# FFN1's end with its updates between quarters of the last block, and a prologue in which k's first tile and x's high parts stand ahead of q's split on ScalarE

## The chip, the cores and the metric

The kernel runs on one core of one Trainium2 chip. The metric is device time in microseconds (us), the median of several executions. Engines are called as in the profile: PE (TensorE matmuls) with PEld (its weight loads), DVE (VectorE), ACT (ScalarE), POOL (GpSimd) and SP (SyncE, which issues the DMAs). Each engine works through its own list of instructions in order and waits on semaphores that the others raise.

## The reference

x is 8 blocks of 128 tokens by 512 features, ctx a second input of the same shape. Four residual layers follow one another, all in float32:

```python
x = x + L0_xattn(layernorm(x), ctx, Wq, Wk, Wv, Wo)     # keys and values from ctx and x, 16 heads of 96
x = x + L0_ffn(layernorm(x), ...)
x = x + L1_xattn(layernorm(x), ctx, Wq, bq, Wkv, bkv, Wo, bo)   # 32 heads of 128
x = x + L1_ffn(layernorm(x), W, b, A, Bmat, LiMEs)

def L1_ffn(x, W, b, A, Bmat, LiMEs):
    H = x @ W.T + b                                   # 512 wide
    z = x @ A                                         # rank 32
    H_slice = H[:, odd tokens, :8]
    delta_slice = z[:, odd tokens] @ LiMEs.T
    logits = 0.5 * H_slice / max|H_slice| + 0.5 * delta_slice / max|delta_slice|
    probs = softmax(logits)
    weights = probs * sigmoid((probs - second_largest(probs)) / 0.5)
    weights = weights / (sum(weights) + 1e-9)
    p_mix = repeat(weights, 2) @ LiMEs                # one weight row for each pair of tokens
    return H + ((z * p_mix) @ Bmat) * 0.5
```

## The kernel before

Tokens lie in 8 blocks of 128. Every float32 matrix product is made as three products of float32r parts: a value is split into a high part (a copy on ACT) and a low part (value minus high part, on DVE or POOL), and PE adds hi x hi, lo x hi and hi x lo in one bank of PSUM. So one 128x128 weight tile against 512 columns is three matmuls (lines 603 to 605), and a full product over 512 features is twelve.

**The prologue** runs from the launch to the first attention head. SP loads, in this order: the first k and v weights (kv_raw), ctx (into qT, in four pieces), x's blocks 0 to 3, the identity and the gate weights, x's blocks 4 to 7, the first q weights (eight pieces, `load_q`, line 526 and 528). ACT splits ctx into cT_hi, DVE and POOL make cT_lo. PE then projects ctx on k and v (`project_context`, four uses u = 0 to 3 of four PSUM banks; u even is k, u odd is v), one k-step at a time for the first two quarters of ctx and with both last quarters at once for the rest. Between these uses it transposes the normalised blocks of x (`transpose_x`, line 831). A block of x goes through: statistics (DVE, line 1677 to 1681), rstd (POOL, line 1421), shift (DVE, line 1686, minus mean times rstd), `normalise_x` (ACT, line 1221), `transpose_x` (PE), `norm_hi` (ACT, line 1226, writes xT_hi), `norm_lo` (DVE, line 1698, writes xT_lo). When blocks 0 to 3 have xT_lo and the bank of context use 0 is evacuated ("kv", 0: ACT lines 1031 and 1043, two instructions), PE projects x on k and v ("kv", 4 and 5), then transposes blocks 5 and 6 and projects on q ("q", 0 to 2). The q weights are split on ACT (line 1020, q0_hi) and POOL (line 1344, q0_lo).

**FFN1's end.** `big_h(b)` makes one block of H (twelve matmuls, four k-steps "quarters" of three); H's blocks 0 to 3 are added to x by `add_h`, those of 4 to 7 stay in PSUM. `z_half` makes z and H's first 8 features, `small` (line 988) the logits of the odd tokens. DVE and ACT then turn logits into weights in a chain of small instructions (lines 1848 to 1892). PE transposes the weights (line 997, wT), multiplies them by LiMEs (line 1001, pmix), DVE multiplies with z (line 1900, zp), ACT and DVE split zp (lines 1333, 1334 and 1906), and PE makes the eight updates ("delta", line 1009): for blocks 4 to 7 into the bank that holds H's block, for 0 to 3 into banks ov and pt in turn. DVE adds an update to x (line 1914), except for blocks 6 and 7, which ACT copies to SBUF (line 1337, moved) and POOL adds (line 1513). SP stores each block of 256 KB when it is added (lines 587, 590 and 593). The order of the updates is written out in one tuple:

```python
DELTAS = (6, 7, 4, 5, 0, 1, 2, 3)
BY_DVE = DELTAS[2:]
```

The loops over heads between these two stretches are not touched.

## Time and profile before

| | us |
|---|---|
| median of 3 runs (lowest, highest) | 1126.47 (1125.64, 1127.51) |
| the profiled execution | 1127.2 |
| its span, first to last instruction | 1125.4 |
| PE busy in it | 1094.7 (97%) |
| DVE, ACT, POOL busy | 545.8, 534.0, 377.8 |

The profiled execution took 1127.2 us, 1.8 us more than its span, and 0.7 us more than the median of the runs. PE is busy for 97% of the span; what it is not busy for lies mostly in the first 27 us and after 1118 us. Two stretches in the record show TensorE's clock at its lower level of 1.2 GHz (half of 2.4 GHz): one in the prologue, one in FFN1's end.

### The profile page before, as it was taken

The numbers are of one execution on the slowest core, as the hardware profiler recorded it, in microseconds if no ns is written. First come the engines' busy times: TensorE is split into PE (matmuls) and PEld (weight loads), VectorE is DVE, ScalarE is ACT, GpSimd is POOL, SyncE is SP. The second block draws the span as 40 slices with busy tenths as digits, with TensorE's granted clock in tenths as the row PEclk, the third lists the DMA queues.
The fourth block names the chain that finished last, engine by engine and source line by source line (L and its number), as shares of the span: only waits on it lengthen the run. The fifth ranks groups of instructions, "written<-read, shape, count | busy, mean of one in ns | idle before, by whom it ended". The sixth has DMA issues, their size and how long they took to land.

```text
span 1125.4 us, 14699 instructions
## 1 busy us (share of the span) xinstructions
PE 1094.7 (97%) x5302; PEld 889.8 (79%) x5302; DVE 545.8 (48%) x1004; ACT 534.0 (47%) x1478; POOL 377.8 (34%) x260
## 2 busy tenths in 40 slices
PE   5999999999999999999999999999999999999997
PEld 4888888887877688877888888888888888888775
DVE  4464366357477532484524435344353352533654
ACT  5475366357477432455616336254262442623741
POOL 3053034025252543476404215033050240512441
PEclk9999999999999999999999999999999999999999
DMA  8111001010000321102021021110210202101002
GB/s 250 24 47 30 1 29 29 1 47 10 1 19 1 103 94 38 38 1 90 25 75 37 4 71 37 64 48 0 75 37 19 93 0 75 37 13 46 15 4 75
DMA packets 31918, 47.88 MB, mean 43 GB/s; under 512 B 19364, under 2 KB 23716, under 8 KB 29188
## 3 DMA queue, kind: packets, MB, share of 16 engines
q1 hardware_dynamic: 31876, 47.33, 13.0%
q8 instruction: 25, 0.41, 0.2%
q14 instruction: 17, 0.14, 0.0%
HBM read 41.02 MB, written 2.10 MB: 38 GB/s over the span
## 4 chain that ended last, share of the span: by engine, by line
PE 89%; ACT 5%; DVE 4%; issue 1%; POOL 1%; DMA 0%; SPq 0%; ACTq 0%; DVEq 0%
PE work L603 15%; PE work L605 14%; PE work L604 14%; PE work L662 8%; PE yb L603 5%; PE yb L604 5%; PE yb L605 5%; PE pt L673 4%; PE ov L603 3%; PE ov L605 3%; PE ov L604 3%; PE pt L605 3%; PE pt L604 3%; PE pt L603 3%; ACT prob L1129 2%; DVE oT_lo L1662 1%
## 5 line engine op out<-in xcount | busy, mean ns | idle before, releaser
L1356 POOL TENSOR_TENSOR prob<-prob,exp_rcp 128x512 f32<-128x512 f32 (+1 forms) x96 | 127.2, 1325 | 534.7 <-DVE exp_rcp L1604 534.7
L1129 ACT ACTIVATE prob<-work,neg_max 128x128 f32<-128x128 f32 (+1 forms) x384 | 149.1, 407 | 65.1 <-DVE neg_max L1629 64.9
L603 PE MATMUL work<-xT_hi,q_hi 128*128 128x512 f32 x416 | 168.1, 404 | 0.4 <-DVE xT_lo L1698 0.4
L605 PE MATMUL work<-xT_hi,q_lo 128*128 128x512 f32 x416 | 164.4, 395 | 0.0
L604 PE MATMUL work<-xT_lo,q_hi 128*128 128x512 f32 x416 | 164.4, 395 | 0.0
L1079 ACT ACTIVATE pT_hi<-pt 128x512 fp32r<-128x512 f32 x128 | 73.8, 602 | 84.4 <-PE pt L673 83.6
L662 PE MATMUL work<-kT,qT 128*128 128x128 f32 (+1 forms) x704 | 112.9, 303 | 0.1
L662 PEld LDWEIGHTS work<-kT,qT 128*128 128x128 f32 (+1 forms) x704 | 102.8, 191 | 11.8 <-issue 0.3
L1662 DVE TENSOR_TENSOR oT_lo<-ov,oT_hi 32x128 fp32r<-32x128 f32 (+2 forms) x160 | 67.4, 421 | 77.7 <-ACT oT_hi L1085 76.4
L1629 DVE TENSOR_REDUCE neg_max<-work 128x4 f32<-128x512 f32 (+1 forms) x96 | 82.8, 863 | 39.7 <-PE work L662 37.8
L1085 ACT ACTIVATE oT_hi<-ov 32x128 fp32r<-32x128 f32 (+2 forms) x160 | 60.2, 376 | 83.7 <-PE ov L605 81.2
L603 PE MATMUL yb<-o_hi,oT_hi 128*128 128x512 f32 x224 | 94.0, 420 | 5.2 <-DVE oT_lo L1662 5.1
L1652 DVE TENSOR_TENSOR pT_lo<-pt,pT_hi 128x512 fp32r<-128x512 f32 x128 | 84.7, 682 | 26.5 <-ACT pT_hi L1079 26.4
L605 PEld LDWEIGHTS work<-xT_hi,q_lo 128*128 128x128 f32 x416 | 78.2, 188 | 18.8
L603 PEld LDWEIGHTS work<-xT_hi,q_hi 128*128 128x128 f32 x416 | 78.3, 188 | 17.8 <-DVE xT_lo L1698 0.6
L604 PEld LDWEIGHTS work<-xT_lo,q_hi 128*128 128x128 f32 x416 | 78.3, 188 | 17.1
L604 PE MATMUL yb<-o_lo,oT_hi 128*128 128x512 f32 x224 | 88.6, 396 | 0.0
L605 PE MATMUL yb<-o_hi,oT_lo 128*128 128x512 f32 x224 | 88.5, 395 | 0.0
L1344 POOL TENSOR_TENSOR o_lo<-raw,o_hi 128x2048 fp32r<-128x2048 f32 (+2 forms) x15 | 62.5, 4170 | 63.8 <-ACT o_hi L1020 63.8
L1129 ACT ACTIVATION_READ_ACCUMULATOR prob<-work,neg_max 128x1 f32 x384 | 81.2, 212 | 0.0
L603 PE MATMUL work<-cT_hi,kv_hi 128*128 128x512 f32 x176 | 70.8, 402 | 10.3 <-DVE cT_lo L1704 10.3
L673 PE MATMUL pt<-ident,prob 128*128 128x128 f32 x512 | 71.5, 272 | 0.0
(216 smaller groups left out, 2103.5 us busy)
## 6 DMA issues: line engine op xcount, KB each, us to landing
raw<-in_l_q SPq DMA_DIRECT2D x8, 1024.0 KB, 5.3
raw<-in_l_o SPq DMA_DIRECT2D x8, 1024.0 KB, 4.7
kv_raw<-in_l_kv SPq DMA_DIRECT2D x8, 515.0 KB, 3.4
prob<-vT SPq DMA_DIRECT2D x128, 32.0 KB, 1.8
raw<-in_l_o SPq DMA_DIRECT2D x4, 768.0 KB, 4.3
raw<-in_l_q SPq DMA_DIRECT2D x16, 144.0 KB, 2.7
qT<-in_ctxT SPq DMA_DIRECT2D x4, 512.0 KB, 5.8
x<-in_x SPq DMA_DIRECT2D x2, 1024.0 KB, 10.3
```

The lines of the kernel that those rows point to most:

```text
L603: pe.matmul(dst, l_hi, r_hi, start=first and k == 0, stop=False)
L604: pe.matmul(dst, l_hi, r_lo, start=False, stop=False)
L605: mm = pe.matmul(dst, l_lo, r_hi, start=False, stop=last and k == n - 1)
L662: mm = pe.matmul(dst[:, g, :], qT[0:L.hd, g, b * P:(b + 1) * P], kT[0:L.hd, b * L.keys:(b + 1) * L.keys] if L.has_v(it) else k3[0:L.hd, b ...
L673: mm = pe.transpose(pt[:, c, g * P:(g + 1) * P], prob[:, b % 2, g * L.keys + c * P:g * L.keys + (c + 1) * P], ident[:, :])
L1079: act.activation(pT_hi[:, c, :], pt[:, c, :], ACT.Copy).then_inc(S.pt_hi_done, 1)
L1129: e = act.activation(prob[:, i % 2, g * L.keys:(g + 1) * L.keys], s[:, g, :], ACT.Exp, bias=neg_max[:, i % 2, g:g + 1], accum_out=exp_sum[ ...
L1344: pool.tensor_tensor(lo[0:rows, 0:n], raw[0:rows, 0:n], hi[0:rows, 0:n].bitcast(F32), ALU.subtract)\
L1356: pool.tensor_tensor(p, p, exp_rcp[:, b % 2, :].unsqueeze(2).broadcast_to([P, G, L.keys]), ALU.mult)\
L1629: dve.tensor_reduce(neg_max[:, b % 2, :], s, AX.X, ALU.max, negate=True).then_inc(S.max_done, 1)
L1652: dve.tensor_tensor(pT_lo[:, c, :], pt[:, c, :], pT_hi[:, c, :].bitcast(F32), ALU.subtract)\
L1662: lower = dve.tensor_tensor(o_buf(L, 1, b)[dst], ov_heads[src], o_buf(L, 0, b)[dst].bitcast(F32), ALU.subtract)
```

## The change

Prologue: ACT makes the high parts of x's blocks 0 to 3 and evacuates k's first tile ("kv", 0) before it splits q, and the gate's split moves behind the last normalisation. PE transposes block 3 one context use earlier. DVE takes the statistics of block 4 ahead of `norm_lo` of blocks 0 to 3. POOL makes q0_lo in two halves with two rstd between. PE gets five matmuls on a constant tile (kT, set by DVE) before its first product; their result is not used.

FFN1's end: the weights' transposes, wT and pmix are made in two halves of 256 columns in two pairs of banks; quarters of H's last two blocks stand between them; the updates of blocks 4, 5, 6 stand behind the first quarter of `big_h(7)`, those of 0 and 1 behind the third, those of 7, 2 and 3 at the end. Updates 2 and 3 go into the banks of H's blocks 4 and 5. Two small DVE instructions of the logits are folded into a scale of the exponential. SP stores in the order 4, 5, 0, 6, 1, 2, 3, 7.

```diff
-        DELTAS = (6, 7, 4, 5, 0, 1, 2, 3)
-        BY_DVE = DELTAS[2:]
+        DELTAS = (4, 5, 6, 0, 1, 7, 2, 3)
+        BY_DVE = (4, 5, 0, 1, 2, 3)
+        MOVED = (6, 7)
+        LOGITS, ABOVE = 8, 8 + 3 + 4 + 1
+
+        def wT_bank(half):
+            return (pt[0:NE, 1, 0:2 * P], ov[0:NE, 0:2 * P])[half]
+
+        def pmix_bank(half):
+            return (pt[0:RANK, 0, 0:2 * P], yb[0:RANK, 0:2 * P])[half]
 
         def delta_bank(b):
+            if b in (2, 3):
+                b += 2
             return work[:, L1.last_bank["h", b], :] if b >= 4 else (ov[:, :], pt[:, 1, :])[b % 2]
...
+            for b in (4, 5, 0, 6, 1, 2, 3, 7):
+                if b in MOVED:
+                    sp.wait_ge(f1.moved_done, MOVED.index(b) + 1)
+                else:
+                    sp.wait_ge(f1.done, BY_DVE.index(b) + 1)
                 sp.dma_start(out[b], x[:, b, :]).then_inc(out_stored, 16)
...
+            pe.wait_ge(warm_set, 1)
+            for _ in range(5):
+                pe.matmul(ov[:, :], kT[:, 0:P], kT[:, 0:HID], start=True, stop=True)
...
             for u in range(4):
                 project_context(u, [2, 3], False, True).then_inc(S0.proj_done, 1)
-                transpose_x(N[0], u, ())
+                for b in ((0,), (1,), (2, 3), ())[u]:
+                    transpose_x(N[0], b, ())
...
-            big_h(6, (0, 1))
+            big_h(6, (0,))
...
+            for n, half in enumerate((1, 0)):
+                big_h(6, (n + 1,))
+                pe.wait_ge(f1.wT_evac, n + 1)
+                pe.matmul(pmix_bank(half), limes[:, :], wT[:, half * 2 * P:(half + 1) * 2 * P], start=True, stop=True)\
+                    .then_inc(f1.pmix, 1)
+            big_h(6, (3,))
+            big_h(7, (0,))
             pe.wait_ge(f1.b_lo, 1)
...
+            for b in DELTAS[:3]:
+                delta(b)
+            big_h(7, (1, 2))
+            for b in DELTAS[3:5]:
+                delta(b)
+            big_h(7, (3,))
+            for b in DELTAS[5:]:
+                delta(b)
...
+            split_lo_part(q0_lo, q_raw, q0_hi, 0, 768, q_hi_done, 0)
+            rstd_of(N[0], 5)
+            rstd_of(N[0], 6)
+            split_lo_part(q0_lo, q_raw, q0_hi, 768, 1536, q_hi_done, 0).then_inc(q_lo_done, 1)
+            rstd_of(N[0], 7)
...
+            dve.memset(kT[:, 0:HID], 1.0).then_inc(warm_set, 1)
...
+            dve.wait_ge(x_loaded[1], 16)
+            statistics(N[0], x, 4)
             for b in range(4):
                 norm_lo(N[0], b)
+            shift(N[0], 4)
             evacuate(L0, S0, 0, ("kv", 3))
...
+            statistics(N[0], x, 5)
+            statistics(N[0], x, 6)
+            shift(N[0], 5)
+            statistics(N[0], x, 7)
+            shift(N[0], 6)
+            shift(N[0], 7)
             norm_lo(N[0], 4)
```

Where the instructions stand, at the places that the prediction speaks of. First ACT in the prologue, behind ctx's split. prob<-x is `normalise_x`, xT_hi is `norm_hi` (blocks 0 and 1 from pt, 2 from ov, 3 from yb), kT and k3 together evacuate one tile of k, q0_hi<-raw is q's split. Before:

```order
L1235 ACTIVATE gate_hi<-gate_raw 128x32 [waits const_loaded]
L1221 ACTIVATE prob<-x,minus_mean,rstd 128x512 [waits ln0_shift] x4
L1020 ACTIVATE q0_hi<-raw 128x1536 [waits q_loaded,q_parts_loaded]
L1226 ACTIVATE xT_hi<-pt 128x4x128 [waits ln0_t] x2
L1226 ACTIVATE xT_hi<-ov 128x4x128 [waits ln0_t]
L1226 ACTIVATE xT_hi<-yb 128x4x128 [waits ln0_t]
L1031 ACTIVATE kT<-work 96x4x128 [waits L0_proj_done]
L1043 ACTIVATE k3<-work 32x4x128
L1031 ACTIVATE kT<-work 96x4x128 [waits L0_proj_done]
L1043 ACTIVATE k3<-work 32x4x128
L1221 ACTIVATE prob<-x,minus_mean,rstd 128x512 [waits ln0_t,ln0_shift] x4
```

And in the change:

```order
L1247 ACTIVATE prob<-x,minus_mean,rstd 128x512 [waits ln0_shift] x4
L1252 ACTIVATE xT_hi<-pt 128x4x128 [waits ln0_t] x2
L1252 ACTIVATE xT_hi<-ov 128x4x128 [waits ln0_t]
L1252 ACTIVATE xT_hi<-yb 128x4x128 [waits ln0_t]
L1057 ACTIVATE kT<-work 96x4x128 [waits L0_proj_done]
L1069 ACTIVATE k3<-work 32x4x128
L1046 ACTIVATE q0_hi<-raw 128x1536 [waits q_loaded,q_parts_loaded]
L1057 ACTIVATE kT<-work 96x4x128 [waits L0_proj_done]
L1069 ACTIVATE k3<-work 32x4x128
L1247 ACTIVATE prob<-x,minus_mean,rstd 128x512 [waits ln0_t,ln0_shift]
L1252 ACTIVATE xT_hi<-pt 128x4x128 [waits ln0_t]
```

q's split has moved behind five other pieces of work, and the normalisation of block 4 (the second prob row) stands alone behind it and behind k's second tile.

Next PE at the program's end. The rows with q_hi and xT are quarters of `big_h(7)`, those with b3 and zp3 are the updates. Before:

```order
L605 MATMUL work<-q_hi,xT_lo 128x512
L603 MATMUL work<-q_hi,xT_hi 128x512
L604 MATMUL work<-q_lo,xT_hi 128x512
L605 MATMUL work<-q_hi,xT_lo 128x512
L1009 MATMUL work<-b3,zp3 128x512 [waits f1_zp_lo,f1_zp_again,f1_b_lo]
L1009 MATMUL work<-b3,zp3 128x512 [waits f1_zp_lo,f1_zp_again] x3
L1009 MATMUL ov<-b3,zp3 128x512 [waits f1_zp_lo,f1_zp_again]
L1009 MATMUL pt<-b3,zp3 128x512 [waits f1_zp_lo,f1_zp_again]
L1009 MATMUL ov<-b3,zp3 128x512 [waits f1_done,f1_zp_lo,f1_zp_again]
L1009 MATMUL pt<-b3,zp3 128x512 [waits f1_done,f1_zp_lo,f1_zp_again]
```

And in the change, from the update of block 4 on, less the first of the two quarters between:

```order
L1026 MATMUL work<-b3,zp3 128x512 [waits f1_zp_lo,f1_zp_again,f1_b_lo]
L1026 MATMUL work<-b3,zp3 128x512 [waits f1_zp_lo,f1_zp_again] x2
...
L611 MATMUL work<-q_hi,xT_hi 128x512
L612 MATMUL work<-q_lo,xT_hi 128x512
L613 MATMUL work<-q_hi,xT_lo 128x512
L1026 MATMUL ov<-b3,zp3 128x512 [waits f1_zp_lo,f1_zp_again]
L1026 MATMUL pt<-b3,zp3 128x512 [waits f1_zp_lo,f1_zp_again]
L611 MATMUL work<-q_hi,xT_hi 128x512
L612 MATMUL work<-q_lo,xT_hi 128x512
L613 MATMUL work<-q_hi,xT_lo 128x512
L1026 MATMUL work<-b3,zp3 128x512 [waits f1_zp_lo,f1_zp_again]
L1026 MATMUL work<-b3,zp3 128x512 [waits f1_done,f1_zp_lo,f1_zp_again] x2
```

The first three updates now stand nine matmuls ahead of the end of `big_h(7)`, and the last two wait for additions of blocks 4 and 5 in place of 0 and 1.

Last DVE at the program's end: wT is the copy of the transposed weights, zp<-zT the product with z, zp3<-zp,zp3 its low part, x<-x the additions. Before:

```order
L1894 COPY wT<-pt 8x512 [waits f1_wT]
L1900 SCALAR_TENSOR_TENSOR zp<-zT,yb 32x512 [waits f1_pmix]
L1900 SCALAR_TENSOR_TENSOR zp<-zT,yb 32x512
L1906 TENSOR_TENSOR zp3<-zp,zp3 32x512 [waits f1_zp_hi] x2
L1914 TENSOR_TENSOR x<-x,work 128x512 [waits f1_b_added,f1_delta] x2
L1914 TENSOR_TENSOR x<-x,ov 128x512 [waits f1_H_added,f1_delta]
L1914 TENSOR_TENSOR x<-x,pt 128x512 [waits f1_H_added,f1_delta]
L1914 TENSOR_TENSOR x<-x,ov 128x512 [waits f1_H_added,f1_delta]
L1914 TENSOR_TENSOR x<-x,pt 128x512 [waits f1_H_added,f1_delta]
```

And in the change:

```order
L1930 COPY wT<-ov 8x256 [waits f1_wT]
L1930 COPY wT<-pt 8x256 [waits f1_wT]
L1937 SCALAR_TENSOR_TENSOR zp<-zT,yb 32x512 [waits f1_pmix]
L1944 TENSOR_TENSOR zp3<-zp,zp3 32x512 [waits f1_zp_hi]
L1937 SCALAR_TENSOR_TENSOR zp<-zT,pt 32x512 [waits f1_pmix]
L1953 TENSOR_TENSOR x<-x,work 128x512 [waits f1_b_added,f1_delta]
L1944 TENSOR_TENSOR zp3<-zp,zp3 32x512 [waits f1_zp_hi]
L1953 TENSOR_TENSOR x<-x,work 128x512 [waits f1_b_added,f1_delta]
L1953 TENSOR_TENSOR x<-x,ov 128x512 [waits f1_H_added,f1_delta]
L1953 TENSOR_TENSOR x<-x,pt 128x512 [waits f1_H_added,f1_delta]
L1953 TENSOR_TENSOR x<-x,work 128x512 [waits f1_H_added,f1_delta] x2
```

The addition of block 4 stands ahead of the second half's low part, and the two halves of zp are no longer made back to back.

## Rows read from the trace of the kernel before

**Rows 1.** The page: the chain that ended last, shares of the span.

```profile
PE 89%; ACT 5%; DVE 4%; issue 1%; POOL 1%; DMA 0%; SPq 0%; ACTq 0%; DVEq 0%
```

**Rows 2.** The chain in the prologue: start us, us, what.

```profile
10.30 0.77 PE work L603
...
13.20 0.43 PE work L603
...
19.18 0.44 PE pt L831 x4
...
24.68 0.45 PE yb L831 x4
...
26.24 0.60 ACT k L1043
26.98 0.47 PE work L603
...
30.66 0.43 PE work L603
31.09 0.24 PE work L604
...
35.66 0.23 PE work L603
```

**Rows 3.** Windows: stretch, us, busy of the five engines, granted clock, DMA.

```profile
30.00:31.00 1.00, 1.00 (x4) 0.77 (x3) 0.96 (x4) 0.74 (x1) 0.55 (x1) 0.51 0.88 189
```

**Rows 4.** Timeline of ACT in the prologue: start us, us, instruction [idle before <-releaser].

```profile
19.49 1.57 ACT L1221 ACTIVATE prob<-x,minus_mean,rstd 128x512 f32<-128x512 f32 x2 [0.26 <-DVE minus_mean L1686]
21.33 1.49 ACT L1020 ACTIVATE q_hi<-raw 128x1536 fp32r<-128x1536 f32 x1 [0.27 <-DMA raw<-in_l_q]
22.73 1.06 ACT L1226 ACTIVATE xT_hi<-pt 128x512 fp32r<-128x512 f32 x2
```

**Rows 5.** Timelines of DVE and POOL in the prologue.

```profile
8.93 2.48 DVE L1704 TENSOR_TENSOR cT_lo<-qT,cT_hi 128x1024 fp32r<-128x1024 f32 x2 [8.93 <-ACT cT_hi L1233]
...
11.57 2.37 POOL L1428 TENSOR_TENSOR cT_lo<-qT,cT_hi 128x1024 fp32r<-128x1024 f32 x1 [3.30 <-ACT cT_hi L1233]
...
13.02 2.00 DVE L1704 TENSOR_TENSOR cT_lo<-qT,cT_hi 128x1024 fp32r<-128x1024 f32 x1 [1.61 <-ACT cT_hi L1233]
...
22.90 3.48 POOL L1344 TENSOR_TENSOR q_lo<-raw,q_hi 128x1536 fp32r<-128x1536 f32 x1 [2.88 <-ACT q_hi L1020]
```

**Rows 6.** Timeline of PE in FFN1's end.

```profile
1112.68 1.04 PE L1001 MATMUL yb<-wT,limes 8*32 8x512 f32 x2
1113.65 0.50 PE L603 MATMUL work<-q_hi,xT_hi 128*128 128x512 f32 x1
...
1116.56 1.09 PE L1009 MATMUL work<-b,zp 96*128 96x512 f32 x4
```

**Rows 7.** Timelines of DVE, ACT and POOL in FFN1's end.

```profile
1113.76 1.28 DVE L1900 SCALAR_TENSOR_TENSOR zp<-zT,yb 32x512 f32<-32x512 f32 x2 [1.69 <-PE yb L1001]
...
1120.60 0.68 DVE L1914 TENSOR_TENSOR x<-x,pt 128x512 f32<-128x512 f32 x1
...
1114.47 0.63 ACT L1333 ACTIVATE zp<-zp 32x512 fp32r<-32x512 f32 x1 [7.39 <-DVE zp L1900]
...
1109.97 1.28 POOL L1509 TENSOR_TENSOR b<-b_raw,b 32x512 fp32r<-32x512 f32 x1 [7.01 <-issue]
1117.77 2.50 POOL L1513 TENSOR_TENSOR x<-x,moved 128x512 f32<-128x512 f32 x2 [6.52 <-ACT moved L1337]
```

**Rows 8.** Tile x from 1110 us: SP's last stores (ns, first and last start), landing.

```profile
L593 SPq DMA_DIRECT2D out<-x x3: 557/642/643, 1120.7 to 1122.0; - x3
...
DMA to landing us min/median/max: 2.0/2.7/3.0
```

**Rows 9.** Windows of 1 us behind the last products, columns as in rows 3.

```profile
1119.00:1120.00 1.00, 0.47 (x1) 0.19 (x1) 0.94 (x3) 0.00 (x0) 1.00 (x2) 1.00 1.00 371
...
1124.00:1125.00 1.00, 0.00 (x0) 0.00 (x0) 0.00 (x0) 0.00 (x0) 0.00 (x0) 0.50 0.55 207
```

More of the change, by code:

```diff
@@ L992, in _, with delta @@
             big_h(5)
-            big_h(6, (0, 1))
+            big_h(6, (0,))
             pe.wait_ge(f1.w, 1)
-            for c in range(AC):
-                mm = pe.transpose(pt[0:NE, 1, c * P:(c + 1) * P], lg[5][:, c, :], ident[:, :])
-            mm.then_inc(f1.wT, 1)
-            big_h(6, (2, 3))
-            pe.wait_ge(f1.wT_evac, 1)
-            pe.matmul(yb[0:RANK, :], limes[:, :], wT[:, :], start=True, stop=True).then_inc(f1.pmix, 1)
-            big_h(7)
+            for n, half in enumerate((1, 0)):
+                for c in (2 * half, 2 * half + 1):
+                    mm = pe.transpose(wT_bank(half)[:, c % 2 * P:(c % 2 + 1) * P], lg[5][:, c, :], ident[:, :])
+                mm.then_inc(f1.wT, 1)
+            for n, half in enumerate((1, 0)):
+                big_h(6, (n + 1,))
[4 more added lines that the diff above has]
+            big_h(7, (0,))
             pe.wait_ge(f1.b_lo, 1)
-            for b in DELTAS:
+            def delta(b):
                 pe.wait_ge(f1.zp_again, 1 if b >= 4 else 2)
@@ L1324, in _, with move @@
             act.activation(b3[:, :], b_raw[:, :], ACT.Copy).then_inc(f1.b_hi, 1)
-            act.wait_ge(f1.dve, 10)
-            act.activation(lg[2][:, :, :], lg[1][:, :, :], ACT.Exp).then_inc(f1.exp, 1)
-            act.wait_ge(f1.dve, 13 + AC + 1)
+            act.wait_ge(f1.dve, LOGITS)
+            act.activation(lg[2][:, :, :], lg[1][:, :, :], ACT.Exp, scale=0.5).then_inc(f1.exp, 1)
+            act.wait_ge(f1.dve, ABOVE)
             act.activation(lg[4][:, :, :], lg[3][:, :, :], ACT.Exp, scale=-2.0).then_inc(f1.exp, 1)
+            def move(n):
+                act.wait_ge(f1.delta, DELTAS.index(MOVED[n]) + 1)
+                act.activation(moved[:, n, :], delta_bank(MOVED[n]), ACT.Copy).then_inc(f1.moved, 1)
             for n, half in enumerate((1, 0)):
@@ L1334, in _ @@
                 act.activation(zp3[AGAIN, at], zp[:, at], ACT.Copy).then_inc(f1.zp_again, 1)
-            for n, b in enumerate(DELTAS[:2]):
-                act.wait_ge(f1.delta, n + 1)
-                act.activation(moved[:, n, :], delta_bank(b), ACT.Copy).then_inc(f1.moved, 1)
+            for n in range(2):
+                move(n)
         @block.gpsimd
@@ L1429, in _ @@
                 .then_inc(c_lo_pool, 1)
-            for b in range(4):
+            for b in range(5):
                 rstd_of(N[0], b)
-            split_lo(q0_lo, q_raw, q0_hi, 1536, P, q_hi_done, q_lo_done, 0)
-            for b in range(4, NB):
-                rstd_of(N[0], b)
+            split_lo_part(q0_lo, q_raw, q0_hi, 0, 768, q_hi_done, 0)
[3 more added lines that the diff above has]
+            rstd_of(N[0], 7)
             pool.wait_ge(f0.gate_split_hi, 1)
@@ L1510, in _ @@
                 .then_inc(f1.b_lo, 1)
-            for n, b in enumerate(DELTAS[:2]):
+            for n, b in enumerate(MOVED):
                 pool.wait_ge(f1.moved, n + 1)
@@ L1712, in _ @@
             evacuate(L0, S0, 0, ("kv", 1))
+            dve.wait_ge(x_loaded[1], 16)
+            statistics(N[0], x, 4)
             for b in range(4):
                 norm_lo(N[0], b)
+            shift(N[0], 4)
             evacuate(L0, S0, 0, ("kv", 3))
-            dve.wait_ge(x_loaded[1], 16)
-            for b in range(4, NB):
-                statistics(N[0], x, b)
-                if b > 4:
-                    shift(N[0], b - 1)
-            shift(N[0], NB - 1)
+            statistics(N[0], x, 5)
[4 more added lines that the diff above has]
+            shift(N[0], 7)
             norm_lo(N[0], 4)
@@ L1871, in _ @@
             chained(dve.tensor_tensor(lg[1][:, :, :], lg[7][:, :, :], per_row(row[3]), ALU.subtract))
[L1872 to L1873 removed]
+            assert step[0] == LOGITS
             dve.wait_ge(f1.exp, 1)
@@ L1882, in _ @@
                                       top8b[:, :, 1:2].broadcast_to([P, AC, NE]), ALU.subtract))
-            assert step[0] == 13 + AC + 1
+            assert step[0] == ABOVE
             dve.wait_ge(f1.exp, 2)
@@ L1907, in _, with add_delta @@
                     .then_inc(f1.zp_lo, 1)
-            for b in BY_DVE:
+            def add_delta(b):
                 dve.wait_ge(f1.delta, DELTAS.index(b) + 1)
@@ L1914, in _ @@
                 dve.tensor_tensor(x[:, b, :], x[:, b, :], delta_bank(b), ALU.add).then_inc(f1.done, 1)
+            gated(0, 1)
+            lower_zp(0, 1)
+            gated(1, 0)
+            add_delta(4)
+            lower_zp(1, 0)
+            for b in BY_DVE[1:]:
+                add_delta(b)
 def laid_out(i):
```

65 lines of the change are left out of this document (29 added, 36 removed).

## The prediction

> **What bounds the kernel now.** I read the page's chain first: 89% of it is PE [rows 1], so a microsecond counts only where PE stands idle or slow, or behind PE's last product. From q's first products (36 us) to 1100 us nothing is changed, and what the prologue gives is carried through as a plain shift. So I read two stretches.
>
> In the prologue the chain runs on PE from 10.30 until block 3 is transposed at 24.68 + 0.45 = 25.13 [rows 2]. Then PE waits until 26.98: k's first tile leaves its bank on ACT only at 26.84, since ACT made q's split of 1.49 us at 21.33, while blocks 0 to 2 stood transposed, and so began x's high parts only at 22.73 [rows 2, 4]. The wait is 1.85 us. It costs more: after it, eight matmuls start 0.43 us apart before the pace of 0.23 comes back at 31.09 [rows 2], and the granted clock there is 0.51, the lower level of 1.2 GHz [rows 3]. Eight times 0.20 is 1.6 us. The first matmuls at 10.30 run at 0.43 too [rows 2].
>
> In FFN1's end all updates stand behind H's last block: the first four begin at 1116.56 [rows 6], DVE ends the last addition at 1120.60 + 0.68 = 1121.28 [rows 7], and SP issues the last store at 1122.0 [rows 8]. From 1119 on the stores move 371 GB/s with the DMA engines' share at 1.00, and they end at about 1124.55 [rows 9]. The output's 2.1 MB at 375 GB/s take 5.6 us, 0.7 us a block, which is all of that time. So the end is set by when the first stores can start, and then by DMA.
>
> **The prologue, step by step.** I walk the new order with the old durations. PE's path to block 0's transpose at 19.18 [rows 2] is kept. Behind it stand six matmuls (1.40), transpose 1 (0.44), six, transposes 2 and 3 (0.88), six: 19.62 + 1.40 + 0.44 + 1.40 = 22.86, transposes to 23.74, end at 25.14. ACT is free at 19.49 + 1.57 = 21.06 [rows 4] and no longer splits q: high part 0 at once, 1 by 22.2, 2 (transposed at 23.30) by 24.0, 3 by 24.55, at 0.53 each (half of the 1.06 of two [rows 4]). k's first tile then takes two instructions, 1.2 us from 25.64 to 26.84 before [rows 2]: 24.55 + 1.2 = 25.75. DVE's low part of block 3 ends at 25.25. So "kv", 4 starts at 25.8 in place of 26.98: **1.2 gained**, PE's wait falls from 1.85 to 0.65. With so short a wait I take the eight slow matmuls as gone: "kv", 4 ends at 28.6 in place of 31.56.
>
> Now what is late next. ACT goes on from 25.75: q's split (1.42 of its pitch) to 27.2, k's second tile (1.2) to 28.4, block 4's normalisation (0.8) to 29.2. PE wants that block at 28.6 and waits 0.6; transpose 4 ends at 29.7, "kv", 5 at 32.5, transpose 5 at 32.95. ACT: high part 4 (0.53), k's third tile (1.2), normalisations 5 and 6 (1.6) end at 33.2, so PE waits another 0.35 for block 6. q's first product starts at 33.75 where it started at 35.66 [rows 2]: **the prologue gives 1.9**. Its q0_lo must be there: POOL's 3.48 [rows 5], now from 27.25 and with two rstd of 0.55 inside, ends at 31.85, 1.9 ahead of need. That is also the margin of everything queued behind q's split on POOL and DVE (rstd 5 to 7, shifts 5 to 7, low part 4). q's DMA landed at 21.33 [rows 4], 4.4 ahead of its new place. The next head's q load is issued behind q0_lo, 5.5 us later than before; its first user comes a whole head later. The gate's split moves with nobody waiting for it.
>
> The bounds: if the shorter waits still bring the slow matmuls, "kv", 4 ends at 30.15, ACT is in time for block 4, block 6 comes at 34.2, and q's product starts at 34.65: 1.0 gained. If the five matmuls on the constant tile make the first context products fast, PE is ready for block 0 at 16.15 + 1.40 = 17.55, block 0 is normalised at 18.15, and everything to "kv", 4 comes 0.85 to 0.95 earlier: 2.8 gained. What these five cost: the one float32 product of 512 columns took about 0.97 until the next matmul [rows 6]; five are 4.9, or 9.7 at half the pace. From about 1.4 (an estimate: the launch and one DVE instruction of 0.7) they end between 6.3 and 11.1, and PE waits until 10.30 anyway: between 0 and 0.8, taken as 0, since only the slowest case costs. DVE's memset lies before its first work at 8.93 [rows 5].
>
> **FFN1's end, step by step**, on the old time axis. PE reaches the weights' transposes after 27 matmuls in place of 30, 0.7 earlier, at 1110.2 (start in the trace: 1112.68 less six matmuls and the transposes). The two DVE instructions saved, 0.2 each, save nothing: the weights are ready before PE asks, now as then. Transposes 0.44, quarter 0.70, pmix (half of 0.97), quarter, pmix, quarter, first quarter of `big_h(7)`: PE stands before update 4 at about 1114.6. pmix 1 is out at 1111.95, so zp (0.64, half of 1.28), ACT's two copies (0.63 each) and the low part (0.68) end by 1114.15 [rows 7]: in time. B's low part is ready at 1111.25 [rows 7], 3.3 ahead. Updates 4, 5, 6 take 0.7, two quarters to 1116.7, updates 0 and 1 (their zp ready at 1116.45) to 1117.2, the last quarter and updates 7, 2, 3 to 1118.6. DVE adds block 4 by 1115.7, 5 by 1117.05, 0 by 1117.8, 1 by 1118.45, 2 by 1119.2, 3 by 1119.85; POOL (1.25 each, of 2.50 [rows 7]) adds 6 by 1118.0 and 7, which PE makes late and ACT must copy, by 1120.2. The last store is block 7's, issued at 1120.3 where the last was issued at 1122.0: 1.7 earlier. By the bytes: block 0's data flows from about 1118.65, and six blocks of 0.69 end at 1122.8 where they ended at 1124.55: 1.75. Both give the same, so **the end gives 1.75**, between 1.4 (SP's issues, up to 0.64 each [rows 8], fall behind each other) and 2.2 (landing at its shortest, 2.0 [rows 8]).
>
> **Two rules beside the rows.** On the waits: a DVE instruction with two SBUF operands took 2.00 while POOL's ran, and 1.24 without [rows 5]. The Trainium skill, "SBUF — State Buffer", Who interferes with whom, calls the port pair of the two engines an exclusive lock, held for a whole instruction. The rows agree: 2.00 is 1.24 plus most of the time until POOL ended. By the rule the new halves of q0_lo hold DVE's shifts 6 and 7 up; by my walk block 6's shift then ends at about 31.9, and ACT asks for it at 32.4, so it moves the chance of the third rival, not the sum.
> On the clock: the slow matmuls stand behind waits of PE, at the start and at 27 us [rows 2]. The Trainium skill, "TensorE: Matmul & The Clock Gate", Part 1, says that half rate is the default, that activity releases it, and that the watch runs free of the kernel's start, so its point moves from run to run. By that rule the five matmuls may serve in one execution and not in the next; the sum by it is the first rival's time.
>
> **The sum.** Against the profiled execution: 1127.2 - 1.9 - 1.75 = 1123.55. That execution lies 0.7 above the median, less than one stretch of eight slow matmuls; the runs shown, 1125.64 to 1127.51, differ by about one. Where before had no slow stretch in the prologue, the change saves less, so I take half of the 0.7 off: **1123.2**, a fall of 3.3 from the median (0.3%). A measurement of this kernel can tell about 0.2% (2.25 us) from no change.
>
> **Rivals.**
> First, the clock is held: the five matmuls carry the higher level over to 10.30. For it: they fill time in which PE is idle. Against: at their fast pace they end up to 4 us before 10.30, and a wait of 1.85 was enough to lose the clock [rows 2]. 1123.2 - 0.9 = 1122.3, chance 0.13.
> Second, the end gives nothing: the stores' bytes are the same, and the new waits inside `big_h(7)` (zp, B's low part, ACT's copy for block 7) hold PE or the last store up by 1.75. Against: margins of 0.3 to 3.3. 1124.9, chance 0.11.
> Third, the prologue gives nothing: ACT becomes the bound. Blocks 4 and 6 arrive late (my walk has 0.6 and 0.35 already), the slow matmuls come back, or q0_lo is late. 1123.2 + 1.9 = 1125.1, chance 0.12.
> Fourth, slower: TensorE's clock falls in FFN1's end and stays down. The change puts six switches between kinds of product there, where two were. From the transposes at 1110.2 to the last update at 1118.6 PE has 8.4 us of work; at 0.43 in place of 0.23 that is 7 more, and the time is 1123.2 + 7 = 1130. It decides from 6 us lost, nearly the whole stretch. Against: the two switches of before lost no clock, the quarter behind pmix started 0.23 paced again at once [rows 6]. Chance 0.04.
> Neither part acts (gains below 0.5 each): 1126, chance 0.03.
> My forecast has 0.57; its own range is 1122.3 to 1124.2.
>
> **How the numbers follow.** Faster by over 0.2% means below 1124.2: nearly all of the forecast (0.54), the first rival (0.13) and the better part of the second and third (0.07): 0.74. Within 0.2%: 0.21. Slower: 0.05. The range from 1121.6 to 1125.3 takes in the first three rivals and leaves out the fourth.
>
> **What would show it.** Right: no q split between x's normalisations and high parts; "kv", 4 about 1.2 earlier, 0.23 apart from its start; q's first product about 1.9 earlier; waits of 0.3 to 0.7 of PE for blocks 4 and 6; the first store near 1115.8 less the shift, the last issue about 10 us after the weights' transposes, a gap between the first stores. Wrong: 0.43 between matmuls from 25 us on; q's product waiting for q0_lo; the stores' end as far behind PE's last matmul as before.

## The result, and the profile after

The changed kernel took 1121.13 us in the median of 5 executions (1120.39 to 1121.47), the kernel before beside it 1126.73 (1125.64 to 1128.30): a ratio of 0.995, 95% interval 0.9938 to 0.9962. That is 5.6 us, where 3.3 were forecast, and 0.5 us under the forecast's range, which begins at 1121.6. The profiled execution took 1121.03 with a span of 1119.2 us. One execution of the kernel before beside the later runs, 1358.98 us at a mean clock of 0.753, is a slow one and is left out of what follows.

In the prologue, the timeline of PE in the changed kernel (start us, us, instruction, idle before and what ended it; "..." leaves rows out here and below):

```profile
1.45 6.73 PE L856 MATMUL ov<-kT 128*128 128x512 f32 x10 [1.45 <-DVE kT L1735]
9.89 0.47 PE L611 MATMUL work<-cT_hi,kv_hi 128*128 128x512 f32 x1 [1.71 <-DVE cT_lo L1738]
10.20 0.39 PE L612 MATMUL work<-cT_lo,kv_hi 128*128 128x512 f32 x1
10.42 0.40 PE L613 MATMUL work<-cT_hi,kv_lo 128*128 128x512 f32 x1
...
18.39 0.66 PE L839 MATMUL pt<-ident,prob 128*128 128x128 f32 x4 [0.89 <-ACT prob L1247]
...
25.07 0.47 PE L611 MATMUL work<-xT_hi,kv_hi 128*128 128x512 f32 x1 [0.52 <-ACT k L1069]
25.38 0.39 PE L612 MATMUL work<-xT_lo,kv_hi 128*128 128x512 f32 x1
...
28.30 0.66 PE L839 MATMUL pt<-ident,prob 128*128 128x128 f32 x4 [0.19 <-ACT prob L1247]
...
32.55 0.47 PE L611 MATMUL work<-xT_hi,q_hi 128*128 128x512 f32 x1
```

The kernel before, at block 0's transposes and at q's first product:

```profile
19.02 0.60 PE L831 MATMUL pt<-ident,prob 128*128 128x128 f32 x4
...
35.42 0.48 PE L603 MATMUL work<-xT_hi,q_hi 128*128 128x512 f32 x1
```

The five constant matmuls (ten passes) end at 8.18, and the first context products, 1.71 us later, already stand 0.23 apart, where [rows 2] has 0.43. "kv", 4 starts at 25.07 (before 26.98) and keeps 0.23, so the slow matmuls behind [rows 2] are gone. The profile's clock doesn't show the slow pace of before's first products. A window of the kernel before, with the granted clock third from the right:

```profile
11.00:12.00 1.00, 1.00 (x4) 0.81 (x3) 0.41 (x1) 0.56 (x2) 0.43 (x1) 1.00 0.95 303
```

Four products fall in it, where six do at 0.23 apart, and the clock is still given as 1.00. So a third slow stretch, at the start, is in no granted clock and in no mean of one; only the distance between matmuls shows it.

The chain of the changed kernel's prologue (start us, us, what):

```profile
5.11 10.19 DMA x<-in_x
...
15.31 0.70 DVE stats L1710
...
17.52 0.82 ACT prob L1247
...
18.39 0.66 PE pt L839 x4
...
24.34 0.59 ACT k L1069
24.93 1.38 ACT q_hi L1046
...
32.79 0.23 PE work L611
```

It begins with x's DMA: PE now waits for block 0, so a still faster start of PE would give nothing. q's first product stands at 32.79, where [rows 2] has 35.66: 2.87 less. By the timelines 0.63 of this is gained up to block 0's transposes (18.39 against 19.02), and 2.24 from there to q's first product (14.16 against 16.40).

In FFN1's end, PE's timeline in the changed kernel, and a window of the granted clock:

```profile
1097.94 1.08 PE L1000 MATMUL pt<-pick,zT 40*128 40x16 f32 x8 [0.88 <-issue]
...
1105.35 0.38 PE L1010 MATMUL ov<-ident,lg 128*8 128x128 f32 x2
...
1110.08 0.86 PE L1026 MATMUL work<-b,zp 96*128 96x512 f32 x3
...
1112.17 0.40 PE L1026 MATMUL ov<-b,zp 96*128 96x512 f32 x1
...
1113.34 0.86 PE L1026 MATMUL work<-b,zp 96*128 96x512 f32 x3
```

```profile
1101.00:1107.00 6.00, 6.00 (x29) 4.19 (x27) 3.82 (x18) 0.46 (x2) 0.49 (x1) 1.00 0.00 0
```

The same window of the kernel before, and its logits' matmuls and transposes of the weights:

```profile
1101.00:1107.00 6.00, 5.90 (x22) 4.92 (x23) 3.33 (x18) 0.38 (x2) 0.38 (x1) 0.72 0.00 0
```

```profile
1101.10 1.09 PE L988 MATMUL pt<-pick,zT 40*128 40x16 f32 x8 [0.88 <-issue]
...
1110.75 0.60 PE L997 MATMUL pt<-ident,lg 128*8 128x128 f32 x4
```

From the logits' matmuls (L988 at 1101.10 before, L1000 now) to the first transposes of the weights, before took 9.65 us (to 1110.75) and the changed kernel 7.41. Three matmuls fewer are 0.70 of that; the other 1.54 is the clock. The stores: SP's issues, and windows of 1 us (the last two numbers are the DMA share and GB/s):

```profile
L601 SPq DMA_DIRECT2D out<-x x8: 332/430/645, 1111.2 to 1115.8; - x8
...
DMA to landing us min/median/max: 2.0/2.5/3.0
```

```profile
1112.00:1113.00 1.00, 1.00 (x6) 0.84 (x5) 1.00 (x2) 0.00 (x0) 1.00 (x1) 1.00 0.70 262
1113.00:1114.00 1.00, 1.00 (x6) 0.63 (x4) 0.89 (x2) 0.22 (x1) 0.30 (x1) 1.00 0.49 184
...
1117.00:1118.00 1.00, 0.00 (x0) 0.00 (x0) 0.00 (x0) 0.00 (x0) 0.00 (x0) 1.00 1.03 387
```

The first store is issued at 1111.2 and the last at 1115.8, 10.45 us behind the transposes (before: 1122.0 - 1110.75 = 11.25, [rows 8]); from there to the end of the span it is 3.4 us in both.

So the 6.2 us between the two spans (1125.4, 1119.2) are: prologue 2.87; slow stretch in FFN1's end 1.54; its three matmuls and its tail 0.70 + 0.80 = 1.50; the remaining 0.3 lies in the unchanged loops between (32.79 to 1097.94 against 35.66 to 1101.10), where no change was forecast.

### The profile page after: what moved, and what is told of

It reads as the page before. It is cut to its first block, busy times and chain, and to the rows that moved or that the text cites. A ratio compares the mean times of both kernels' runs of the same rounds, so it can differ in the third digit from the quotient of the medians.

```text
span 1119.2 us, 14724 instructions
## 1 busy us (share of the span) xinstructions
PE 1097.1 (98%) x5314; PEld 888.9 (79%) x5314; DVE 547.2 (49%) x1004; ACT 534.2 (48%) x1478; POOL 378.4 (34%) x261
## 4 chain that ended last, share of the span: by engine, by line
PE 87%; ACT 5%; DVE 4%; DMA 1%; issue 1%; POOL 1%; SPq 0%; POOLq 0%; ACTq 0%; DVEq 0%
PE work L611 14%; PE work L613 14%; PE work L612 14%; PE work L670 8%; PE yb L611 5%; PE yb L612 5%; PE yb L613 5%; PE pt L681 4%; PE ov L611 3%; PE ov L613 3%; PE ov L612 3%; PE pt L613 3%; PE pt L612 3%; PE pt L611 3%; ACT prob L1155 2%; DVE oT_lo L1695 1%
```

## The experiments

My theory: the five constant matmuls, taken as worth nothing, are worth about 1 us; and the slow stretch in FFN1's end follows PE's pause ahead of the logits, comes in some executions and not in others, and was missing here by luck. The rivals: the stretch is gone because of the change; the order alone made the prologue; the end is set by something other than the stores' rate.

Times and ratios are against the kernel before, in executions on the same chip. The clock is the mean over an execution. It counts the fall behind PE's last product, and it doesn't count the slow pace at the start. In the profiled executions of all these kernels the granted clock falls, ahead of PE's last products, only in the two stretches known from before: with one the mean is 0.997 or 0.998 (a, c, f, g), with both 0.996 (b). But l has neither and stands at 0.998 too, since its clock is at 0.50 from 1118 us to the end at 1123.1. So 0.999 or 1.000, called a full clock here, tells that neither stretch was there; a lower mean alone doesn't tell that one was, and is read together with the span. Only one execution of each kernel has a trace. a to d, e to h, i to k, and l ran on four chips; the fastest span of before on each is 1123.1 to 1123.3.

| kernel | median us | ratio (95%) | clock and spans of its executions |
|---|---|---|---|
| a_no_warm | 1123.23 | 0.9966 (0.9954 to 0.9978) | 3 at 1.000: 1119.9 to 1120.5; 3 at 0.998: 1122.3 to 1122.7 |
| b_warm_only | 1125.60 | 0.9985 (0.9976 to 0.9994) | 11 at 0.995 to 0.998: 1121.7 to 1124.7 |
| c_order_only | 1125.36 | 0.9985 (0.9976 to 0.9994) | 12 at 0.996 to 0.999: 1121.2 to 1124.5 |
| d_end_only | 1123.99 | 0.9981 (0.9972 to 0.9990) | 6 at 1.000: 1121.8 to 1122.4; 5 at 0.996 or 0.997: 1122.2 to 1124.6 |
| e_after_again | 1122.50 | 0.9960 (0.9947 to 0.9974) | 1 at 1.000: 1119.1; 4 at 0.997 or 0.998: 1120.4 to 1121.2 |
| f_before_fill | 1124.68 | 0.9981 (0.9972 to 0.9990) | 11 at 0.997 or 0.998: 1122.5 to 1123.8 |
| g_put_back | 1122.27 | 0.9957 (0.9944 to 0.9971) | 1 at 1.000: 1119.6; 4 at 0.997 or 0.998: 1120.5 to 1121.2 |
| h_half_stores | 1120.20 | 0.9942 (0.9928 to 0.9956) | 2 at 1.000: 1117.5, 1117.6; 3 at 0.998 or 0.999: 1118.4 to 1119.6 |
| i_after_fill | 1120.75 | 0.9951 (0.9937 to 0.9964) | 5 at 0.999 or 1.000: 1118.7 to 1119.1 |
| k_after_fill_gated | 1120.43 | 0.9950 (0.9937 to 0.9964) | 4 at 0.999 or 1.000: 1118.3 to 1118.8; 1 at 0.997: 1119.6 |
| j_warm_2 | 1123.37 | 0.9974 (0.9965 to 0.9983) | 2 at 1.000: 1119.1, 1119.7; 8 at 0.995 to 0.998: 1120.3 to 1122.7 |
| l_before_pause_filled | 1124.87 | 0.9982 (0.9973 to 0.9991) | 11 at 0.998 or 0.999: 1122.3 to 1124.1 |

The kernel before stood at 0.994 to 0.998 in the 72 other executions beside these runs, with spans of 1123.1 to 1126.5.

**Parts of the change.** `a_no_warm` is the changed kernel without the constant tile's matmuls:

```diff
-            pe.wait_ge(warm_set, 1)
-            for _ in range(5):
-                pe.matmul(ov[:, :], kT[:, 0:P], kT[:, 0:HID], start=True, stop=True)
...
-            dve.memset(kT[:, 0:HID], 1.0).then_inc(warm_set, 1)
```

> The change without the five matmuls on the constant tile and without DVE's memset. Theory A (the five matmuls hold TensorE's clock from 10 us on, the new order alone gives 1.9 us): the first context products run 0.43 apart again, q's first product starts near 33.7 us in place of 32.8, and the median is 1122.1. If FFN1's end then shows its slow stretch again (theory A2: the five matmuls also decide that), 1123.6. Rival B (the order alone gave all of the 2.9 us, the five matmuls nothing): 1121.1, q's first product near 32.8.

`b_warm_only` is the kernel before with these lines alone (with +).

> The kernel before with the five matmuls and the memset alone. Theory A: context products 0.23 apart from the start, but ACT's q split still holds k's first tile, so kv 4 starts near 26.2 us in place of 27.0, behind a wait of about 1.9 us; the median falls by 0.8 to 1125.9, or more if the eight slow matmuls behind that wait are gone too (1124.3). Rival B: no change, 1126.7.

`c_order_only` is the kernel before with the prologue's new order alone; on ACT:

```diff
-            evacuate(L0, S0, 0, *L0.ahead_all[0:4])
...
+            evacuate(L0, S0, 0, ("kv", 0))
             act.wait_ge(q_parts_loaded, (2 * KT - 1) * 16)
             split_hi(q0_hi, q_raw, 0, 1536, P, q_loaded, None, 0, 0).then_inc(q_hi_done, 1)
+            evacuate(L0, S0, 0, ("kv", 2))
```

> The kernel before with the prologue's new order on PE, ACT, DVE and POOL alone, no five matmuls, FFN1's end as before. Theory A: q's first product at 33.7 us, a gain of 1.9, median 1124.8. Rival B: a gain of 2.9, median 1123.8.

`d_end_only` is the kernel before with all edits of FFN1's end and none of the prologue's:

```diff
-        DELTAS = (6, 7, 4, 5, 0, 1, 2, 3)
+        DELTAS = (4, 5, 6, 0, 1, 7, 2, 3)
...
```

> The kernel before with FFN1's end changed alone. The prediction's term, corrected by the trace of the change: 1.5 us from the updates between the quarters, so 1125.2. If the slow stretch behind the logits' matmuls goes with FFN1's new order (rival C), 1.6 more: 1123.6, and the trace shows 0.23 between all matmuls of that stretch. If it stays as in the trace of before, it is not the new order in FFN1's end that removed it.

The stages of the traces, by PE's starts (us; block 0's transposes, q's first product, the logits' matmuls, the weights' transposes, the end of the span):

| trace | to block 0 | to q | to the logits | to the weights | to the end |
|---|---|---|---|---|---|
| before | 19.02 | 16.40 | 1065.68 | 9.65 | 14.65 |
| changed | 18.39 | 14.16 | 1065.39 | 7.41 | 13.85 |
| a_no_warm | 19.92 | 14.07 | 1065.85 | 8.96 | 13.90 |
| c_order_only | 19.46 | 14.11 | 1065.63 | 9.66 | 14.64 |
| d_end_only | 19.55 | 15.13 | 1065.90 | 7.40 | 13.82 |
| l_before_pause_filled (below) | 19.43 | 15.15 | 1065.72 | 8.12 | 14.68 |

The constant matmuls act up to block 0: 18.08 to 18.86 in the seven traces with five of them, 18.60 to 19.92 in the six without any, 1.0 between the means. It is 0.63 between before and the changed kernel, since before's slow pace at the start lasts eight matmuls, and 1.53 between a, where it lasts fourteen, and the changed kernel. The spans at full clock (a 1119.9 to 1120.5, the changed kernel 1118.6 to 1119.7) also give 1.0. The order acts from block 0 to q: 1.0 where the clock holds there (a and c against d and l), and 2.24 where before had its slow matmuls. The end's edits give 1.5 from the logits' matmuls to the end at full clock (l 1100.30 to 1123.1, the changed kernel 1097.94 to 1119.2). The loops take 1065.28 to 1065.40 in the eight traces with constant matmuls (two in j) and 1065.63 to 1065.90 in the six without; nothing was changed there, and why they differ isn't known.

Of the medians, b gains 1.8 on the 1127.43 of before beside it, c 2.1 and d 3.4, where 0.8, 1.9 and 1.5 were expected; d's surplus is its executions without a stretch, b's is in no trace. a's 1123.23 lies between the values expected without and with FFN1's stretch, 1122.1 and 1123.6, as its executions do. d's 1123.99 is near the 1123.6 expected if the end's new order took FFN1's stretch away, but a and the changed kernel (below) have that order and the stretch. In the profiled execution of c the pause ahead of "kv", 4 is 0.52 us and 25 to 36 us stands at 1.00; in b it is 2.06 and the slow matmuls are back. In d it is as long as in before and the clock held: the pause allows the fall, it doesn't force it. Why six of eleven executions of d had no stretch at all, with both pauses of before, stays open.

FFN1's end shows the same, a pause that loses the clock in one execution and not in another. PE in `a_no_warm`:

```profile
1099.84 1.08 PE L997 MATMUL pt<-pick,zT 40*128 40x16 f32 x8 [0.88 <-issue]
...
1101.42 0.43 PE L613 MATMUL work<-q_hi,xT_lo 128*128 128x512 f32 x1
1101.65 0.62 PE L611 MATMUL work<-q_hi,xT_hi 128*128 128x512 f32 x1
1102.07 0.63 PE L612 MATMUL work<-q_lo,xT_hi 128*128 128x512 f32 x1
```

The code of FFN1's end and the pause of 0.88 are those of the changed kernel, where no matmul is slow. From the logits to the transposes it is 8.96 here and 7.41 there: 1.55.

**Luck or change.** `e_after_again` is the changed kernel with no edit.

> The changed kernel once more, with nothing altered, beside the kernel before, to see whether the full clock in FFN1's end belongs to it or was luck. If the change itself keeps the clock up there (PE starts 3 us earlier, and its warm-up shifts what the clock's watch sees), every execution shows a mean granted clock of 0.999 to 1.000 and a span within 0.6 us of 1119.2. If the slow stretch comes and goes by execution, as it did in the kernel without the five constant matmuls (3 executions of 6 at 0.998 and 2.3 us longer), some executions stand at 0.998 with spans of 1120.7 to 1121.5, and the median rises by up to 1.5 us.

Not the change: by clock and span four executions of five have the stretch, and the median is 1122.50, where the first five executions of the same kernel had none. Of the ten, six stand at 0.999 or above (spans 1118.6 to 1119.7) and four below (1120.4 to 1121.2). That it was chance alone is not shown: the record names no chip for the first five, and g, nearly the same kernel on the chip of e, has it in four of five as well.

**The pause in FFN1's end, filled.** `f_before_fill` is the kernel before with:

```diff
+            big_h(4, (0,))
             pe.wait_ge(ffn1_loaded, 7 * 16)
             pe.wait_ge(f1.z_evac, 2)
...
-            big_h(4)
+            big_h(4, (1, 2, 3))
...
-            big_h(6, (0, 1))
+            big_h(6, (0, 1, 2))
...
-            big_h(6, (2, 3))
+            big_h(6, (3,))
```

> The kernel before, with one edit: the first quarter of H's block 4 (three matmuls, 0.7 us) runs ahead of the wait for z's evacuation, where PE pauses 0.88 us, and the quarters behind it move up by one, so that PE is idle about 0.2 us there. If that pause is what lets the clock fall in FFN1's end, the stretch at 0.72 there is gone in every execution: 1101 to 1107 us at 1.00, some 1.6 us off the kernel before, and 0.2 to 0.7 us more because one quarter less stands behind the logits: 1125.0 to 1125.6. If the fall doesn't hang on this pause, the granted clock there is 0.72 as before, and the time is 1126.7 to 1127.2.

PE and the clock in its FFN1's end:

```profile
1100.67 1.08 PE L989 MATMUL pt<-pick,zT 40*128 40x16 f32 x8 [0.18 <-issue]
1101.68 0.50 PE L603 MATMUL work<-q_hi,xT_hi 128*128 128x512 f32 x1
1102.02 0.39 PE L604 MATMUL work<-q_lo,xT_hi 128*128 128x512 f32 x1
```

```profile
1101.00:1107.00 6.00, 6.00 (x30) 1.00 0.00 0
```

All 11 executions lie within 1.3 us at 0.997 or 0.998: the trace has the prologue's stretch left, and the means of 0.994 to 0.996 that before shows are gone. 2.5 us in the median were saved, a little more than expected; in the traces 2.07 from the logits to the end (22.23 against 24.30), of which 1.54 is the stretch. Right behind the pause stand the eight small matmuls of the logits (1.0 us); no run varied these, so that they share in the fall isn't ruled out.

**The pause in the prologue, filled.** `l_before_pause_filled` is the kernel before with six matmuls whose result nobody reads:

```diff
+            pe.wait_ge(N[0].lo, 1)
+            product(pt[:, 0, :], list(zip(weights(kv_hi, kv_lo, 2 * P, 0, P)[:2],
+                                          columns(cT_hi, cT_lo, 0, HALF)[:2])))
             pe.wait_ge(N[0].lo, 4)
```

> The kernel before, with six matmuls more whose result nobody reads, in PE's pause of 1.85 us ahead of the product kv 4 of the prologue; all waits and the order stay, so kv 4 still waits for k's first tile until about 26.98. If PE's pause is what lets the clock fall there, the matmuls behind it start 0.23 us apart in place of 0.43, 25 to 36 us stands at 1.00, and that alone is worth 1.6 us where before had the stretch: about 1125.5 in the median, with the stretch in FFN1's end left to come and go. If the fall hangs on something else there (the switch from transposes to products, or the stretch's place), the eight slow matmuls stay, and the time is that of before, 1126.5 to 1127.2.

Its PE behind the pause:

```profile
26.56 0.40 PE L605 MATMUL pt<-cT_hi,kv_lo 128*128 128x512 f32 x1
27.42 0.47 PE L603 MATMUL work<-xT_hi,kv_hi 128*128 128x512 f32 x1 [0.47 <-ACT k L1046]
27.73 0.39 PE L604 MATMUL work<-xT_lo,kv_hi 128*128 128x512 f32 x1
27.96 0.40 PE L605 MATMUL work<-xT_hi,kv_lo 128*128 128x512 f32 x1
```

"kv", 4 starts no earlier than in before (ACT's evacuation still ends the wait), but at 0.23. No execution is below 0.998. Work that does nothing is worth 2.4 us in the median, more than the eight matmuls' 1.6. In the trace 1.25 is gained from block 0 to q, since PE then waits a little for block 4, and 1.53 in FFN1's end, which was at full clock too, though its pause of 0.88 was not touched. The spans of all 11 lie within 1.8 around this execution's 1123.1, so few of them can have FFN1's stretch. So the pause ahead of the logits isn't all that decides on it; how the prologue bears on it stays open.

**How much ahead of the first product.** `j_warm_2` is the changed kernel with `for _ in range(2)`.

> The changed kernel with two constant matmuls at its start in place of five; they end at about 4.2 us, 5.7 us ahead of the first context product (with five: 8.18, 1.71 us ahead). In the changed kernel the constant matmuls themselves got faster about 4 us after the first of them. If the clock rises only behind that much work, or is not held over the longer wait, the first context products stand 0.43 us apart, as without any, and the prologue takes about 1.0 us longer: full-clock spans of 1120.0 to 1120.5 against 1118.6 to 1119.7. If two are enough, 0.23 apart and no longer.

```profile
1.45 3.78 PE L856 MATMUL ov<-kT 128*128 128x512 f32 x4 [1.45 <-DVE kT L1735]
10.48 0.77 PE L611 MATMUL work<-cT_hi,kv_hi 128*128 128x512 f32 x1 [5.25 <-DVE cT_lo L1738]
11.05 0.63 PE L612 MATMUL work<-cT_lo,kv_hi 128*128 128x512 f32 x1
...
13.86 0.39 PE L613 MATMUL work<-cT_hi,kv_lo 128*128 128x512 f32 x1
```

Two are not enough in this execution: the first products are 0.43 apart until 13.6. But its full-clock spans, 1119.1 and 1119.7, lie below the 1120.0 to 1120.5 expected. The slow pace lasts seven matmuls here, and PE comes to block 0 at 18.98, 0.59 behind the changed kernel; so the 1.0 us is a mean, and the price hangs on how long an execution starts slowly. Its other means (0.995 with spans of 1120.3 to 1122.4, 0.998 with 1122.6 and 1122.7) don't follow the spans and tell no stretches apart. Whether the shorter work or the longer wait kept the clock down stays open.

**The two small instructions.** `g_put_back` is the changed kernel with:

```diff
+            chained(dve.tensor_scalar(row[2][:, 0:2], row[1][:, 0:2], 1.0, None, ALU.mult))
...
+            chained(dve.tensor_scalar(lg[1][:, :, :], lg[1][:, :, :], 1.0, None, ALU.mult))
```

> The changed kernel with the two small VectorE instructions of the router's logits put back (a scaling of two numbers a row, here by 1.0, and a multiplication of 128x32 values by 1.0): 0.20 and 0.22 us from start to start. If VectorE's chain of logits sets the time at which PE may transpose the weights (its last value was there 0.07 us ahead of PE at full clock), PE waits 0.35 us there and the kernel takes 0.3 to 0.4 us longer, about 1121.5. If PE sets it, as the prediction had it, nothing: 1121.1.

The profiled execution has the slow stretch, and there the weights are ready at 1105.42, 1.22 ahead of PE (timeline of DVE and PE):

```profile
1105.23 0.19 DVE L1929 TENSOR_TENSOR lg<-lg,row 128x32 f32<-128x32 f32 x1
...
1106.64 0.38 PE L1010 MATMUL ov<-ident,lg 128*8 128x128 f32 x2
```

In the changed kernel at full clock they are ready at 1105.27, 0.08 ahead of 1105.35:

```profile
1105.08 0.19 DVE L1927 TENSOR_TENSOR lg<-lg,row 128x32 f32<-128x32 f32 x1
```

So their price hangs on the clock: nothing with the stretch (spans 1120.5 to 1121.2 against 1120.4 to 1121.2). Without it the two traces give an estimate of 0.33: the weights are ready 7.74 behind the logits' matmuls in g (1097.68), and PE asks for them 7.41 behind. The one such execution, 1119.6 against 1119.2 (the mean of six), fits and can't prove it.

**The stores.** `h_half_stores` leaves out half of every output block:

```diff
-                sp.dma_start(out[b], x[:, b, :]).then_inc(out_stored, 16)
+                sp.dma_start(out[b, :, 0:HID // 2], x[:, b, 0:HID // 2]).then_inc(out_stored, 16)
```

> The changed kernel, with the left half of each output block stored only, so that half of the output isn't written. The last store is issued at the same time, 1115.8 us. If the transfers' rate sets the end (375 to 389 GB/s over the last 4 us), the queue is never full with half the bytes, and the end comes 1.0 to 1.6 us earlier: a span of 1117.6 to 1118.2. If the end is the last store's own latency (3.4 us from its issue to the end of the span in both kernels), the span falls by 0.3 us or less.

```profile
L601 SPq DMA_DIRECT2D out<-x x8: 332/374/447, 1110.8 to 1115.3; - x8
...
DMA to landing us min/median/max: 1.7/1.7/1.8
```

In the trace 1.3 us are gained from the weights' transposes to the end (12.54 against 13.85; the spans at full clock fall by 1.6), and from the last issue to the end it is 2.2 in place of 3.4: 1.2 of these 3.4 us go with the halved bytes, the rest is left of the last store's own way. The rate sets the end, but only for its last part.

**A better version.** `i_after_fill` is the changed kernel with the first quarter of block 4 in the pause, and no quarter between the two halves of pmix:

```diff
+            big_h(4, (0,))
             pe.wait_ge(ffn1_loaded, 7 * 16)
...
-            big_h(6, (0,))
+            big_h(6, (0, 1))
...
-                big_h(6, (n + 1,))
+                if n == 0:
+                    big_h(6, (2,))
```

> The changed kernel with the same edit that took the slow stretch out of the kernel before: the first quarter of H's block 4 runs in PE's 0.88 us pause ahead of the logits, each later quarter up to the weights' transposes moves up by one, and one quarter fewer stands between the two halves of the mixing product. If the pause decides on the clock, every execution shows a mean granted clock of 0.999 or 1.000, and the spans lie together at 1118.5 to 1119.0 (the full-clock executions of the changed kernel, 1118.6 to 1119.7, less 0.2 to 0.5 for the quarter): 1120.3 to 1120.8. If the fall came from elsewhere, some executions stay at 0.997 or 0.998 and 1.5 us above that.

`k_after_fill_gated` moves one line of VectorE more:

```diff
-            lower_zp(0, 1)
             gated(1, 0)
+            lower_zp(0, 1)
```

> The kernel above with one more edit on VectorE: the gated product of the second half of z goes ahead of the lower part of the first half, into the 0.7 us in which VectorE waits for ScalarE's high part. The updates of blocks 0 and 1 can then start about 1 us earlier than at 1112.17, and the first 2 us of the stores, at 262 and 184 GB/s in the changed kernel, fill up. If the transfers' rate sets the end, a span of 1117.7 to 1118.3, 1119.5 to 1120.1; if the last block's update and its store's latency set it, 0.2 or less below the kernel above.

i does what was expected: five executions within 0.5 us. From the logits' matmuls to the end of the span it takes 20.70 us (1098.30 to 1119.0) where the changed kernel took 21.26. k takes 20.70 too (1097.60 to 1118.3), so its edit gives nothing. Its PE shows why:

```profile
1109.09 0.94 PE L1028 MATMUL work<-b,zp 96*128 96x512 f32 x3 [0.22 <-DVE zp L1946]
1111.26 0.40 PE L1028 MATMUL ov<-b,zp 96*128 96x512 f32 x1
```

zp's lower part is ready at 1111.00, but update 0 stands behind two quarters in PE's list and starts at 1111.26, 13.66 us behind the logits, as in i. Both are faster than before; against the changed kernel i gains 0.5 us in the tail, and none of its five executions has the stretch that cost the changed kernel some 1.6 us in four executions of ten (mean spans of 1120.85 and 1119.2). Five are few to show that it is gone for good, and where k's one execution at 0.997 lost its clock isn't known.

## Why the prediction was partly right

**The five constant matmuls: the step that failed.** The prediction took them as worth nothing and gave "the clock is held" 0.13, arguing that at their fast pace they would end up to 4 us ahead and that 1.85 us had been enough to lose the clock. They ran at the slow pace for most of the way (windows of 1 us hold two passes each up to 5 us, three in the next, then four), ended at 8.18, and the pace of 0.23 was held over 1.71. Nor does a wait of 1.85 always lose the clock: d's 1.86 kept it, and so did a pause of 2.51 behind the constant matmuls of i. In the traces they are worth 1.0 us up to block 0 in the mean, 0.63 between before and the changed kernel. What set block 0's transposes then was its normalisation (18.15 in the first rival's walk, 18.33 in the trace), and behind that x's DMA, which no step named. The first rival's sum comes out nearly to the row, 2.8 against 2.87 for the prologue, but partly by luck: it had 0.9 of it from these matmuls and 1.9 from the order, where the traces have 0.63 and 2.24.

**FFN1's slow stretch: the step that was missing.** "On the old time axis" kept the matmuls of 1102 to 1106 at 0.43 without saying so, as a fixed cost. It is one that comes and goes: 1.55 us, absent, by their clocks, in the five executions that gave the result, and present in four of the next five (the traced execution of g, the same kernel but for two small instructions, has its one stretch there). With all four terms as measured the sum becomes 1127.2 - 2.87 - 1.54 - 1.50 - 0.3 = 1121.0. This term is the largest part of the miss, and that it was absent is not the change's doing: the second five executions, at 1122.50, lie inside the forecast's range and near the first rival's 1122.3. The 0.3 in the loops was in no step either; it comes with the constant matmuls in every trace, and its cause stays open.

**The order of the prologue: right, a little too small.** 1.9 were forecast, and from block 0 to q the traces of before and the changed kernel give 2.24: 1.0 is the order alone, the rest the slow matmuls, which can be missing without it too (in d's trace, and in l's with its pause filled). "kv", 4 waits 0.52 (0.65 forecast) and the slow matmuls are gone, as assumed. Block 4 is waited for 0.19 in place of 0.6 and block 6 not at all: ACT was a little faster than the walk. q0_lo was in time.

**The end: right, a little too large.** 1.75 forecast, 1.50 measured. Update 4 starts 4.73 us behind the transposes. The walk says 4.4, though its own terms add up to 4.2. It had 0.70 for a quarter ahead of either half of pmix and 0.49 for a half; from start to start the trace has 0.88 and 0.90 (1105.70 to 1106.58, 1107.12 to 1108.02), and 0.54 and 0.55. Experiment i, with one quarter fewer there, gets 0.5 back. That transfers set the end is borne out by h for 1.2 us of it.

**"Save nothing": right by the old clock only.** The two small instructions are hidden behind PE while its matmuls are slow. At full clock DVE is 0.08 us ahead, and g suggests a price of 0.3 to 0.4.

**The other rivals** failed: no update waited in the end, and the clock stood at 1.00 over all switches between kinds of product. ACT does lead the chain from 22.76 to 28.25, as the third rival had it, but PE's waits for it are only 0.52 and 0.19.

## What to carry to other kernels

Before a time axis is carried over, look whether matmuls on it run at the lower clock, and behind which pause: that cost belongs to the pause and to chance, and a prediction needs it as a term with a share of executions. Fill PE's short waits with work that is due anyway (a quarter of the next block's product moved ahead of the wait); it cost nothing here, and even useless matmuls paid. Compare stages of traces and executions with the same mean clock before crediting an edit, and read the pace at the start from the distance between matmuls: the granted clock is given as 1.00 there in all of these traces.
